# Output projection node tile by node tile, with four resident weight quarters, inside the edge-count build

## The chip, the cores and the metric

The kernel runs on one core of one Trainium2 chip. Its time is the device time of one launch in microseconds (us); below 2211.28 us for the kernel before, the median of three runs. TensorE (PE) multiplies matrices, VectorE (DVE), ScalarE (ACT) and GpSimd (POOL) do elementwise work, SyncE (SP) here only issues DMAs. Each engine works through its own list of instructions in order and waits on semaphores where the code says so.

## The reference, cut to what matters

Two layers over 1250 nodes with 1024 features and 20000 edges. The part that the change touches is in layer 0: the attention output is normalized, multiplied by a 1024x1024 matrix and added to the node features, and a second branch multiplies the features by a graph matrix built from the edges.

```python
h = jnp.einsum('nd,od->no', x, W) + b            # L0 gnn; self edges are appended to row and col
deg = jnp.zeros((num_nodes,), dtype=h.dtype).at[row].add(1.0)
norm = deg_inv_sqrt[row] * deg_inv_sqrt[col]
out = jax.ops.segment_sum(norm[:, None] * h[col], row, num_segments=num_nodes)
...
normed = (out - mu) / jnp.sqrt(var + EPS) * gamma + beta      # L0 mix
return normed @ W_out + b_out
```

All products are made in float16 pairs: an operand is split in a high and a low part, and each product is three matmuls (high-high, high-low, low-high).

## The kernel before

The nodes are 10 tiles of 128 (`NT`, `TN`), the features 8 blocks of 128 (`KD`). The stage in question, from about 776 us to 962 us of the span, does two things side by side:

- The edge-count build. The sorted edges come in 118 slices (`NST`). For each slice PE multiplies one-hot matrices (4 matmuls, "a stage" of the loop here, `st`); ACT copies the result out of PSUM (`rw`, counted by `rows_out`); DVE adds it to the count matrix `Bc` (`add_rows`, counted by `b_free`). DVE also makes the one-hots, for two stages at a time (`hot`, five instructions, counted by `oh_ready`).
- The output projection. One unit is one node tile times one quarter of `W_out` (256 columns): 24 matmuls of 128x256. There are 40 units, named u. `OUTS_AT` lists after which stage each stands. PE makes it into bank 2 or 3 of PSUM, DVE adds it to `X` (a "unit sum", counted by `evac`).

A weight quarter is loaded as float32 into `wst` by SP (`load`, which waits on `w_split` until the quarter before has been split), copied to float16 high by ACT (`weights_high`) and made into the low part by DVE (`weights_low`, which counts `w_split`). There are two slots for split quarters, so the order of the units is quarter by quarter: ten node tiles for quarter 0, then ten for quarter 1, and so on.

Ahead of the first stage ACT and POOL each clear half of `Bc` (`bc_clear`). After the last stage a serial chain leads to the next stage, the gather (`agg0`): DVE sums the degrees and adds two count rows (`both`), PE transposes them (`turn`), DVE scales (`make`), ACT and POOL split the result in `ATh` and `ATl`, and PE begins the gather with 60 matmuls for each node tile. The gather reads `G0`, 5 MB that SP loads in one DMA once all 40 units are through, since it lies where the projection's input `OT0h`, `OT0l` lay.

The order of all of it is written by hand in the code of each engine. SP's queue has the loads in program order too, and each waits for those ahead of it to be issued.

Of the kernel before, what the change touches and what calls it, by code (L numbers as in the profile page):

```python
# [8 lines left out]
F16 = mybir.dt.float16  # L9
# [3 lines left out]
ALU = mybir.AluOpType  # L13
# [95 lines left out]
def build_program(nc, A, out):  # L109

    with ExitStack() as ctx:
# [204 lines left out]
        z_normed, z_gained = sem("z_normed"), sem("z_gained")  # L316
        gb_loaded, g_hi, g_back = sem("gb_loaded"), sem("g_hi"), sem("g_back")
        g_saved = [sem(f"g_saved{r}") for r in range(4)]
# [18 lines left out]
        b_loaded = sem("b_loaded")  # L337
        xr_loaded = [sem(f"xr_loaded{i}") for i in range(NT)]
        x_biased = sem("x_biased")
# [176 lines left out]

        def unit(pe, n, t, o, xh, xl, i):
# [3 lines left out]
            at = slice(i * TN, (i + 1) * TN)  # L521
            x, m = three(o, [(xh[:, k, at], xl[:, k, at], Wh[:, k], Wl[:, k]) for k in range(KD)])
            if t % NT == 0:
                x.then_inc(slot_begun, 1)
            m.then_inc(mm_done, 1)

        def g_unit(pe, u):
            T = TILE0["gnn0"] + u
            wait_ring(pe, T)
            unit(pe, SLOT0["gnn0"] + u // NT, u, ps[0:TN, T % 4, 0:256], XTh, XTl, u % NT)  # L530

# [340 lines left out]
        def _(pe):  # L872
# [61 lines left out]
            def gather(i, c):  # L934
                s, T = i % 2, T0 + 2 * i + c
                if c == 0:
                    pe.wait_ge(at_lo, i + 1)
                wait_ring(pe, T)
                _, m = three(ps[0:TN, T % 4, :],
                             [(ATh[s][:, k], ATl[s][:, k], G0[:, 0, k, c * 512:(c + 1) * 512],  # L940
                               G0[:, 1, k, c * 512:(c + 1) * 512]) for k in range(NT)])
                m.then_inc(mm_done, 1)
# [22 lines left out]
            turn(0)  # L965
            pe.wait_ge(g_back, 16)
            for i in range(NT - 1):
# [262 lines left out]
        def _(act):  # L1230
# [199 lines left out]
        def _(pool):  # L1430
# [217 lines left out]
        def _(sp):  # L1648
# [3 lines left out]
            for i in range(NT):  # L1652
                if i == NT - 1:
                    sp.wait_ge(const_ready, 1)
                sp.dma_start(X[0:rows_of(i), i], x_rows(i)).then_inc(xr_loaded[i], 16)
                if i == 1:
# [56 lines left out]
            sp.dma_start(bias_g, A["L0_gnn_b"].unsqueeze(0).to_broadcast([TN, DIM])).then_inc(gb_loaded, 16)  # L1713
            sp.wait_ge(b_loaded, 32)
            sp.dma_start(bias_o, A["L0_mix_b_out"].unsqueeze(0).to_broadcast([TN, DIM])).then_inc(b_loaded, 16)
            sp.wait_ge(fold_out, NGR)
            sp.dma_start(es.rearrange("p j q c -> p (j q) c").rearrange("p (t q) c -> p t q c", q=2),
                         edges_d.rearrange("(t p q) c -> p t q c", p=128, q=2)).then_inc(e_back, 16)
            for i in range(NT):
# [4 lines left out]
                if i in (1, 3):  # L1724
                    load(sp, 14 + i // 2, wst[:, 0:2048], A["w_gnn0"][2 + i // 2])
                if i == 6:
                    load(sp, 16, wst[:, 0:2048], A["w_out0"][0])
                sp.wait_ge(turn_done, TURN0["lnO"] + i + 1)
                sp.dma_start(X[0:rows_of(i), i], x_rows(i)).then_inc(xr_loaded[i], 16)
            for n in (17, 18, 19):  # L1730
                load(sp, n, wst[:, 0:2048], A["w_out0"][n - SLOT0["mix0_out"]])
            load(sp, SLOT0["ffn_up"], wsti[:, 0:2048], A["w_up0"][0])
            sp.wait_ge(mm_done, TILE0["agg0"])
# [78 lines left out]
        def _(dve):  # L1812
# [161 lines left out]
            for i in range(NT):  # L1974
                dve.wait_ge(z_gained, i + 1)
                zz = z[i % 2][:, 0:DIM]
                v.tensor_tensor(zz, zz, bcast[1], ALU.add).then_inc(z_ready, 1)
                if i in (0, 3, 6, 8):
                    weights_low(dve, 13 + (i + 1) // 3)
                for u in range(4 * i, 4 * i + 4):  # L1980
                    g_sum(u)
# [4 lines left out]
                g_low(4 * i + 3)  # L1986
                turn_lows(dve, "lnO", i, i % 2, OT0h, OT0l, OS0)
                if i == NT - 4:
# [8 lines left out]
            def add_rows(st):  # L1997
# [4 lines left out]
                rows = flat[:, bass.ds(off, BW)]  # L2002
                v.tensor_tensor(rows, rows, rw[st % 4], ALU.add).then_inc(b_free, 1)
            hot(1)
            dve.wait_ge(bc_clear, 2)
            dve.wait_ge(st_moved, 16)
            for st in range(NST):
                if st % 2 == 0 and st // 2 + 2 < NST // 2:
                    hot(st // 2 + 2)
                if st in OUTS_AT:  # L2010
                    u = OUTS_AT.index(st)
                    if u < NT:
                        dve.wait_ge(xr_loaded[u], 32)
                    dve.wait_ge(mm_done, TILE0["mix0_out"] + u + 1)
                    x = X[:, u % NT, u // NT * 256:u // NT * 256 + 256]
                    stt(x, out_bank(u), 1.0 / (OS0 * WS), x, ALU.mult, ALU.add).then_inc(evac, 1)
# [506 lines left out]
```

## Time and profile before

| | |
|---|---|
| time, median of 3 runs (lowest to highest) | 2211.28 us (2209.93 to 2212.87) |
| profiled execution, first to last instruction (span) | 2207.7 us |
| PE busy | 2068.7 us, 94% |
| DVE busy | 1234.6 us, 56% |
| ACT busy | 725.6 us, 33% |
| POOL busy | 1003.1 us, 45% |

The page gives the profiled execution as its span only; what lies around the span is the 3.6 us by which the median of the runs exceeds it. A share is an average over all stages. The stage of the change has other shares than the whole.

### The profile page before, as it was taken

Reading aid. Unit: us, or ns where it says so; the run is one execution under the profiler, and the core shown is the slowest. Engines: PE = TensorE matmul, PEld = TensorE weight load, DVE = VectorE, ACT = ScalarE, POOL = GpSimd, SP = SyncE. Lnnn points to the kernel's source line nnn. Section 1 sums busy time; section 2 is a strip of 40 time slices with the busy share of each in tenths; the row PEclk is TensorE's granted clock in tenths of the full one; section 3 lists DMA queues with packets and bytes.
Section 4 is the critical chain, followed back from the end, with each engine's and each line's share of the span. In section 5 each row is a group of like instructions: output and inputs, shape, how many; then the busy total and the mean of one; then the engine's idle time right before and its main releaser. Section 6 shows DMA issues by size and latency. Waiting matters only on the chain.

```text
span 2207.7 us, 41128 instructions
## 1 busy us (share of the span) xinstructions
PE 2068.7 (94%) x16448; PEld 1423.1 (64%) x16448; DVE 1234.6 (56%) x2250; ACT 725.6 (33%) x1080; POOL 1003.1 (45%) x783
## 2 busy tenths in 40 slices
PE   7989999999998999969999999999999998977997
PEld 6555564474457977734545577747877887865765
DVE  6784555547566699965534622546555633374332
ACT  5243444435563354320230512312222220052332
POOL 3218777878773200025503873049334422333554
PEclk9999999999999999979999999999999999987999
DMA  4302333324156311060001021211211212376886
GB/s 160 89 20 56 87 91 74 91 69 104 23 140 158 113 54 39 13 200 20 20 0 47 28 73 38 88 39 34 66 41 40 55 29 63 140 304 180 153 153 106
DMA packets 128120, 182.14 MB, mean 83 GB/s; under 512 B 52066, under 2 KB 97257, under 8 KB 121679
## 3 DMA queue, kind: packets, MB, share of 16 engines
q1 hardware_dynamic: 111102, 150.87, 22.6%
q0 software_dynamic: 16848, 28.90, 7.8%
q8 instruction: 119, 1.95, 0.4%
q14 instruction: 51, 0.41, 0.1%
HBM read 120.82 MB, written 53.49 MB: 79 GB/s over the span
## 4 chain that ended last, share of the span: by engine, by line
PE 76%; POOL 9%; DVE 6%; issue 5%; DMA 2%; ACT 1%; SPq 0%; DVEq 0%; POOLq 0%; ACTq 0%
PE ps L494 19%; PE ps L497 19%; PE ps L496 19%; POOL edges_sorted L1532 4%; PE pt L717 2%; DVE RB L798 2%; PE ps L699 2%; PE pt L912 2%; PE pt L479 1%; POOL WR L1524 1%; POOL WR L1523 1%; POOL WR L1520 1%; PE pt L1155 1%; PE ps L1174 1%; PE ps L1175 1%
## 5 line engine op out<-in xcount | busy, mean ns | idle before, releaser
L494 PE MATMUL ps<-WR,RB 128*128 128x256 f16 (+2 forms) x2248 | 630.2, 280 | 6.9 <-DVE SR L1817 3.5
L496 PE MATMUL ps<-WR,RB 128*128 128x256 f16 (+2 forms) x2248 | 629.8, 280 | 0.0
L497 PE MATMUL ps<-WR,RB 128*128 128x256 f16 (+2 forms) x2248 | 629.7, 280 | 0.0
L494 PEld LDWEIGHTS ps<-WR,RB 128*128 128x128 f16 x2248 | 220.2, 98 | 52.7 <-DVE RB L446 3.1
L494 PE MATMUL ps<-RB,WR 128*128 128x512 f16 (+1 forms) x720 | 246.5, 342 | 8.0 <-DVE RB L446 7.4
L1532 POOL DMA_INDIRECT edges_sorted<-SR x160 | 199.9, 1250 | 117.4 <-DVE SR L1922 56.9
L497 PEld LDWEIGHTS ps<-WR,RB 128*128 128x128 f16 x2248 | 220.0, 98 | 42.5 <-issue 0.7
L497 PE MATMUL ps<-RB,WR 128*128 128x512 f16 (+1 forms) x720 | 246.4, 342 | 0.0
L496 PE MATMUL ps<-RB,WR 128*128 128x512 f16 (+1 forms) x720 | 246.4, 342 | 0.0
L496 PEld LDWEIGHTS ps<-WR,RB 128*128 128x128 f16 x2248 | 220.5, 98 | 39.7 <-issue 0.8
L1473 POOL TENSOR_TENSOR WR<-WR,units 128x3072 f32<-128x3072 f32 (+2 forms) x16 | 74.2, 4635 | 371.5 <-PE ps L494 317.3
L798 DVE SCALAR_TENSOR_TENSOR RB<-ps,SR 128x1024 f16<-128x1024 f32 (+2 forms) x120 | 121.5, 1022 | 45.0 <-ACT SR L760 44.4
L760 ACT ACTIVATE SR<-ps 128x1024 f16<-128x1024 f32 (+2 forms) x120 | 104.3, 869 | 88.7 <-PE ps L699 64.7
L2234 DVE TENSOR_TENSOR SR<-SR 128x128 f32<-128x128 f32 (+2 forms) x104 | 101.0, 971 | 44.8 <-ACT SR L1359 44.8
L1476 POOL TENSOR_TENSOR WR<-WR,units 128x3072 f16<-128x3072 f32 (+2 forms) x20 | 90.6, 4530 | 71.2 <-PE ps L494 48.9
L699 PE MATMUL ps<-RB 64*128 64x512 f16 (+2 forms) x960 | 111.7, 339 | 11.5 <-DVE RB L798 10.1
L1630 POOL DMA_INDIRECT out<-WR,SR x54 | 84.4, 1563 | 82.3 <-ACT WR L1412 69.3
L494 PEld LDWEIGHTS ps<-RB,WR 128*128 128x128 f16 x720 | 71.0, 99 | 66.9 <-issue 9.9
L460 ACT ACTIVATE SR<-RB,nbias,rstd 128x1024 f32<-128x1024 f32 x50 | 61.7, 1237 | 144.1 <-POOL nbias L441 144.1
L497 PEld LDWEIGHTS ps<-RB,WR 128*128 128x128 f16 x720 | 71.0, 99 | 57.7 <-issue 1.6
L496 PEld LDWEIGHTS ps<-RB,WR 128*128 128x128 f16 x720 | 71.0, 99 | 57.2 <-issue 1.4
L1520 POOL TENSOR_TENSOR WR<-WR,units 128x512 f32<-128x512 f32 x64 | 69.0, 1078 | 81.8 <-DMA WR<-in_w_moe 81.4
(348 smaller groups left out, 4041.9 us busy)
## 6 DMA issues: line engine op xcount, KB each, us to landing
WR<-in_w_moe SPq DMA_DIRECT2D x64, 256.0 KB, 3.6
moe_split<-WR SPq DMA_DIRECT2D x128, 128.0 KB, 1.8
RB<-moe_split SPq DMA_DIRECT2D x8, 2048.0 KB, 15.6
WR<-in_w_mix SPq DMA_DIRECT2D x12, 1024.0 KB
WR<-in_w_mix SPq DMA_DIRECT2D x8, 1536.0 KB
RB<-in_x SPq DMA_DIRECT2D x18, 512.0 KB, 6.1
WR<-in_w_out SPq DMA_DIRECT2D x8, 1024.0 KB
RB<-counts SPq DMA_DIRECT2D x10, 640.0 KB, 4.8
```

What stands on the lines that cost most here:

```text
L494: m = nc.tensor.matmul(o, ah, bh, start=(k == 0), stop=False)
L496: nc.tensor.matmul(o, ah, bl, start=False, stop=False)
L497: m = nc.tensor.matmul(o, al, bh, start=False, stop=(k == n - 1))
L699: m = nc.tensor.matmul(bank[0:r, h, 0:w], k[HEAD[h], keys], x[HEAD[h], q], start=(n == 0), stop=(n == 2))
L760: nc.scalar.activation(Ph[u % 6][0:r, :, 0:w], score_bank(T, j)[0:r, :, 0:w], ACT.Relu).then_inc(hi_done, 2)
L798: nc.vector.scalar_tensor_tensor(Pl[u][0:r, :, 0:w], score_bank(T, j)[0:r, :, 0:w], 0.0, Ph[u][0:r, :, 0:w], ALU.max, ALU.subtract).then_i ...
L1473: ch.link(g.tensor_tensor(w, w, units[:, 2:3].to_broadcast([128, width]), ALU.mult))
L1476: ch.link(g.tensor_tensor(wh[s][:, 0:width], wst[:, 0:width], units[:, 3:4].to_broadcast([128, width]), ALU.mult))
L1520: ch.link(g.tensor_tensor(pst[s], pst[s], units[:, 2:3].to_broadcast([128, PIECE]), ALU.mult))
L1532: g.indirect_dma_start(edges_d, bass.IndirectOffsetOnAxis(pos[:, t:t + 1], 0), rec[:, t, :], None).then_inc(e_moved, 16)
L1630: g.indirect_dma_start(out2, bass.IndirectOffsetOnAxis(idx2[:, c, t:t + 1], 0), yo[t % 3][:, c * 512:(c + 1) * 512], None, compute_op=ALU. ...
L2234: v.tensor_tensor(o, vw(er[e]), vw(er[2 + e]), ALU.add).then_inc(k_done, 1)
```

## The change

`OUTS_AT` now has 36 entries, from stage 8 on, 2.75 stages apart (before: 40 entries from stage 1 on, 2.5 apart). The last four units stand behind the loop, on PE ahead of the first `turn`, and on DVE their sums stand between the two `both`, ahead of `make(0)`. A unit number u means node tile u // 4 and quarter u % 4, so the first four units need all four quarters. Quarters 0 to 3 lie in spare halves of the weight slots, in the two slots, and in the end and the beginning of `wst` itself.

The conversions therefore move to the front: the high copy of quarter 1 stands on ACT before its clear of `Bc`, that of quarter 2 after stage 1 and that of quarter 3 after stage 6; DVE makes the low parts before its wait for `bc_clear`, after stage 3 and after stage 8.

`OT0h` and `OT0l` are laid out by node tile, so that when the four units of a node tile are through, the 512 KB of `G0` for that tile can be loaded over them. SP issues ten such loads in place of the one. The load of the output bias and that of the next stage's weights move behind these ten, since `wst` is in use until the last unit.

```diff
-OUTS_AT = [5 * u // 2 + 1 for u in range(4 * NT)]
+OUTS_AT = [8 + 11 * u // 4 for u in range(4 * NT - 4)]
...
-        OT0h, OT0l = R2(0, F16, KD, NP), R2(20480, F16, KD, NP)
+        OT0h, OT0l = R2(0, F16, NT, KD, TN), R2(20480, F16, NT, KD, TN)
...
+        tails = WR(12288, F16, 2, 2, 3072)[:, :, :, 2048:3072]
...
+        def quarter(c):
+            if c == 0:
+                return tails[:, 0], tails[:, 1]
+            if c == 3:
+                return (wst_h.rearrange("p (b n) -> p b n", b=2) for wst_h in (WR(8192, F16, 2048), WR(0, F16, 2048)))
+            return (w[c - 1][:, 0:2048].rearrange("p (b n) -> p b n", b=2) for w in (wh, wl))
+
+        def quarter_high(act, c):
+
+            act.wait_ge(w_loaded, 16 * (SLOT0["mix0_out"] + c) + 16)
...
+        def out_unit(pe, u):
+
+            i, c = divmod(u, 4)
+            if u < 4:
+                pe.wait_ge(w_split, SLOT0["mix0_out"] + c + 1)
+            if u >= 2:
+                pe.wait_ge(evac, TILE0["mix0_out"] + u - 1)
...
                 if st in OUTS_AT:
-                    u = OUTS_AT.index(st)
-                    if u >= 2:
-                        pe.wait_ge(evac, T0 + u - 1)
-                    unit(pe, SLOT0["mix0_out"] + u // NT, u, out_bank(u), OT0h, OT0l, u % NT)
+                    out_unit(pe, OUTS_AT.index(st))
+            for u in range(4 * NT - 4, 4 * NT):
+                out_unit(pe, u)
...
-                if i in (2, 5, 7):
+                if i in (2, 5):
                     weights_high(act, 14 + i // 3)
+                if i == 7:
+                    quarter_high(act, 0)
+            quarter_high(act, 1)
...
-                if st - 1 in (OUTS_AT[0], OUTS_AT[NT], OUTS_AT[2 * NT]):
-                    weights_high(act, 17 + OUTS_AT.index(st - 1) // NT)
+                if st == 1:
+                    quarter_high(act, 2)
+                if st == 6:
+                    quarter_high(act, 3)
...
-            sp.dma_start(G0, g0_d).then_inc(g_back, 16)
+            for i in range(NT):
+                sp.wait_ge(mm_done, TILE0["mix0_out"] + 4 * i + 4)
+                sp.dma_start(G0[:, :, i], g0_d[:, :, i]).then_inc(rows_loaded[i], 16)
+            sp.wait_ge(b_loaded, 32)
+            sp.dma_start(bias_o, A["L0_mix_b_out"].unsqueeze(0).to_broadcast([TN, DIM])).then_inc(b_loaded, 16)
+            load(sp, SLOT0["ffn_up"], wsti[:, 0:2048], A["w_up0"][0])
...
             hot(1)
+            quarter_low(dve, 1)
             dve.wait_ge(bc_clear, 2)
...
-                if st - 3 in (OUTS_AT[0], OUTS_AT[NT], OUTS_AT[2 * NT]):
-                    weights_low(dve, 17 + OUTS_AT.index(st - 3) // NT)
+                if st == 3:
+                    quarter_low(dve, 2)
+                if st == 8:
+                    quarter_low(dve, 3)
...
             both(0)
-            both(1)
+            for u in range(4 * NT - 4, 4 * NT - 2):
+                out_sum(u)
             dve.wait_ge(dis_ready, 1)
...
+            both(1)
+            for u in range(4 * NT - 2, 4 * NT):
+                out_sum(u)
             make(0)
```

ACT at the front of the loop, before. The clear of `Bc` is the row of 128x6400, a copy of a stage's result has 128x626, and a high copy of a weight quarter 128x2048.

```order
L1266 ACTIVATE RB<-pt 128x8x128 [waits turn_done]
L1272 ACTIVATE RB<-kvs 128x6400 [waits mm_done]
L1280 ACTIVATE SR<-ps 128x626 [waits g_saved3,g_saved2,oh_used,g_saved1,g_saved0]
L1280 ACTIVATE SR<-pt 128x626 [waits oh_used] x2
L598 ACTIVATE WR<-WR 128x2048 [waits w_loaded,slot_begun]
L1280 ACTIVATE SR<-ps 128x626 [waits oh_used]
L1280 ACTIVATE SR<-pt 128x626 [waits b_free,oh_used] x2
```

And now:

```order
L1304 ACTIVATE RB<-pt 128x1024 [waits turn_done]
L544 ACTIVATE WR<-WR 128x2048 [waits slot_begun,w_loaded]
L1314 ACTIVATE RB<-kvs 128x6400 [waits mm_done]
L1322 ACTIVATE SR<-ps 128x626 [waits g_saved3,g_saved2,oh_used,g_saved1,g_saved0]
L1322 ACTIVATE SR<-pt 128x626 [waits oh_used]
L544 ACTIVATE WR<-WR 128x2048 [waits mm_done,w_loaded]
L1322 ACTIVATE SR<-pt 128x626 [waits oh_used]
L1322 ACTIVATE SR<-ps 128x626 [waits oh_used]
L1322 ACTIVATE SR<-pt 128x626 [waits b_free,oh_used] x2
L1322 ACTIVATE SR<-ps 128x626 [waits b_free,oh_used]
L544 ACTIVATE WR<-WR 128x2048 [waits mm_done,w_loaded]
```

A high copy (L544) now stands ahead of the clear; a second one stands behind the copy of stage 1 and a third behind the copy of stage 6, each waiting on `w_loaded`.

DVE behind the last stage, before. The first row is the last `add_rows`; the 128x1250 rows are `both`, the 128x1024 row is the first part of `make(0)`.

```order
L2003 TENSOR_TENSOR RB<-RB,SR 128x626
L2022 TENSOR_REDUCE deg<-RB 128x10 [waits b_free]
L2023 TENSOR_SCALAR deg<-deg 128x10 [waits dve_chain]
L2025 MEMSET SR 128x30
L2025 MEMSET SR 128x30 [waits dve_chain]
L2031 TENSOR_TENSOR SR<-RB 128x1250 [waits turn_done,dve_chain]
L2031 TENSOR_TENSOR SR<-RB 128x1250 [waits turn_done]
L2069 TENSOR_SCALAR deg<-deg 128x10 [waits dis_ready]
L2070 TENSOR_SCALAR deg<-deg 128x10 [waits dve_chain]
L2038 TENSOR_TENSOR SR<-pt,deg 128x1024 [waits turn_done,dve_chain]
```

And now, from the row behind the last `add_rows` on:

```order
L2077 TENSOR_REDUCE deg<-RB 128x10 [waits b_free]
L2078 TENSOR_SCALAR deg<-deg 128x10 [waits dve_chain]
L2080 MEMSET SR 128x30
L2080 MEMSET SR 128x30 [waits dve_chain]
L2086 TENSOR_TENSOR SR<-RB 128x1250 [waits turn_done,dve_chain]
L1862 SCALAR_TENSOR_TENSOR RB<-ps,RB 128x256 [waits mm_done,rows_loaded9]
L1862 SCALAR_TENSOR_TENSOR RB<-ps,RB 128x256 [waits mm_done]
L2125 TENSOR_SCALAR deg<-deg 128x10 [waits dis_ready]
L2126 TENSOR_SCALAR deg<-deg 128x10 [waits dve_chain]
L2086 TENSOR_TENSOR SR<-RB 128x1250 [waits turn_done,dve_chain]
L1862 SCALAR_TENSOR_TENSOR RB<-ps,RB 128x256 [waits mm_done] x2
L2093 TENSOR_TENSOR SR<-pt,deg 128x1024 [waits turn_done]
```

Four unit sums (128x256) have come in between `both(0)` and `make(0)`, two ahead of `both(1)` and two behind it.

SP from the last load of node features on, before:

```order
L1729 DMA RB<-in_x 98x1024 [waits turn_done]
L385 DMA WR<-in_w_out0 128x2048 [waits w_split] x3
L385 DMA WR<-in_w_up0 128x2048 [waits w_split]
L1736 DMA RB<-g0_split 128x20480 [waits g_saved2,g_saved1,g_saved3,g_saved0,mm_done]
L1739 DMA counts<-RB 2560x2x625 [waits deg_ready,b_free]
```

And now:

```order
L1771 DMA RB<-in_x 98x1024 [waits turn_done]
L386 DMA WR<-in_w_out0 128x2048 [waits w_split] x2
L1778 DMA RB<-g0_split 128x2x1024 [waits g_saved3,g_saved2,mm_done,g_saved1,g_saved0]
L1778 DMA RB<-g0_split 128x2x1024 [waits mm_done] x9
L1780 DMA WR<-in_L0_mix_b_out 128x1024 [waits b_loaded]
L386 DMA WR<-in_w_up0 128x2048 [waits w_split]
L1784 DMA counts<-RB 2560x2x625 [waits deg_ready,b_free]
```

One quarter fewer is loaded here, the load of `G0` is in ten parts, each waiting for its units, and the bias and the `w_up0` load stand behind them and ahead of the store of the counts.

## Rows read from the trace of the kernel before

**Rows 1.** The page, its first line.
```profile
span 2207.7 us, 41128 instructions
```

**Rows 2.** Busy time by windows: whole loop: length; PE, PEld, DVE, ACT, POOL; clock, DMA share, GB/s.
```profile
776.50:961.94 185.44, 173.60 (x1432) 129.71 (x1432) 175.01 (x451) 84.58 (x122) 2.25 (x1) 0.96 0.15 55
```

**Rows 3.** Groups by line, DVE in that window: count, busy us, mean ns, idle before, releasers.
```profile
L2003 DVE TENSOR_TENSOR RB<-RB,SR 128x626 f16 x118 | 56.9, 482 | 9.3 <-DVE RB L2003 7.8 <-issue 0.9 <-ACT SR L1280 0.5
...
L1817 DVE SCALAR_TENSOR_TENSOR RB<-ps,RB 128x256 f32<-128x256 f32 x40 | 16.7, 418 | 0.2 <-PE ps L497 0.2
L603 DVE SCALAR_TENSOR_TENSOR WR<-WR 128x2048 f16<-128x2048 f32 x3 | 6.9, 2285 | 0.0
```

**Rows 4.** Timeline, DVE in the loop: start us, duration us, engine, line, operation.
```profile
827.20 0.49 DVE L2003 TENSOR_TENSOR RB<-RB,SR 128x626 f16 x1 [0.20 <-DVE RB L2003]
...
831.58 0.48 DVE L2003 TENSOR_TENSOR RB<-RB,SR 128x626 f16 x1
...
915.94 0.49 DVE L2003 TENSOR_TENSOR RB<-RB,SR 128x626 f16 x1 [0.20 <-DVE RB L2003]
...
919.12 0.49 DVE L2003 TENSOR_TENSOR RB<-RB,SR 128x626 f16 x1 [0.20 <-DVE RB L2003]
...
946.06 0.48 DVE L2003 TENSOR_TENSOR RB<-RB,SR 128x626 f16 x1
946.74 0.49 DVE L2003 TENSOR_TENSOR RB<-RB,SR 128x626 f16 x1 [0.20 <-DVE RB L2003]
...
948.92 0.48 DVE L2003 TENSOR_TENSOR RB<-RB,SR 128x626 f16 x1
```

**Rows 5.** Timeline of all engines where the loop begins.
```profile
775.08 5.53 ACT L1272 ACTIVATE RB<-kvs 128x6400 f32<-128x6400 f32 x1
...
775.94 15.30 SPq L385 DMA_DIRECT2D WR<-in_w_out  x2
...
776.98 2.82 DVE L1972 TENSOR_SCALAR SR<-SR 128x625 f16<-128x625 f16 x4
...
780.51 0.68 ACT L1280 ACTIVATE SR<-ps 128x626 f16<-128x626 f32 x1
...
782.43 0.47 DVE L2003 TENSOR_TENSOR RB<-RB,SR 128x626 f16 x1
...
782.99 1.91 ACT L598 ACTIVATE WR<-WR 128x2048 f16<-128x2048 f32 x1 [0.64 <-DMA WR<-in_w_out]
```

**Rows 6.** Timeline, SP and ACT: one weight quarter loaded alone and its copy.
```profile
660.09 0.33 SPq L385 DMA_DIRECT2D WR<-in_w_gnn  x1
...
665.10 1.91 ACT L598 ACTIVATE WR<-WR 128x2048 f16<-128x2048 f32 x1 [2.72 <-DMA WR<-in_w_gnn]
```

**Rows 7.** Timeline of all engines where the loop ends and the gather begins.
```profile
957.84 1.25 PE L912 MATMUL ps<-SR 128*128 128x512 f16 x4
...
961.45 0.49 DVE L2003 TENSOR_TENSOR RB<-RB,SR 128x626 f16 x1 [0.33 <-DVE RB L2003]
...
962.62 2.83 DVE L2031 TENSOR_TENSOR SR<-RB 128x1250 f32<-128x1250 int16 x2
...
964.18 2.37 PE L930 MATMUL pt<-ident,SR 128*128 128x128 f32 x10 [5.09 <-issue]
...
966.23 1.23 DVE L2038 TENSOR_TENSOR SR<-pt,deg 128x1024 f32<-128x1024 f32 x1 [0.49 <-PE pt L930]
...
972.29 0.61 PE L494 MATMUL ps<-RB,SR 128*128 128x512 f16 x1 [2.32 <-POOL SR L1562]
```

**Rows 8.** Busy time and granted clock by windows of 2 us, near the end.
```profile
942.00:944.00 2.00, 1.43 (x6) 0.64 (x7) 1.80 (x7) 0.50 (x2) 0.00 (x0) 0.51 1.06 451
976.00:978.00 2.00, 2.00 (x10) 0.91 (x9) 0.06 (x1) 0.07 (x1) 1.85 (x1) 0.96 1.08 254
```

**Rows 9.** Timeline, PE within a unit: first matmul of two successive threes.
```profile
934.88 0.27 PE L494 MATMUL ps<-WR,RB 128*128 128x256 f16 x1
...
935.21 0.27 PE L494 MATMUL ps<-WR,RB 128*128 128x256 f16 x1
```

More of the change, by code:

```diff
@@ L337, in build_program @@
         b_loaded = sem("b_loaded")
-        xr_loaded = [sem(f"xr_loaded{i}") for i in range(NT)]
+        rows_loaded = [sem(f"rows_loaded{i}") for i in range(NT)]
         x_biased = sem("x_biased")
@@ L515, in gemm_nodes, with g_unit @@
                     m.then_inc(mm_done, 1)
-        def unit(pe, n, t, o, xh, xl, i):
+        def g_unit(pe, u):
+            T, n, at = TILE0["gnn0"] + u, SLOT0["gnn0"] + u // NT, slice(u % NT * TN, (u % NT + 1) * TN)
+            wait_ring(pe, T)
             pe.wait_ge(w_split, n + 1)
             Wh, Wl = (w[n % 2][:, 0:2048].rearrange("p (k n) -> p k n", k=KD) for w in (wh, wl))
-            at = slice(i * TN, (i + 1) * TN)
-            x, m = three(o, [(xh[:, k, at], xl[:, k, at], Wh[:, k], Wl[:, k]) for k in range(KD)])
-            if t % NT == 0:
+            x, m = three(ps[0:TN, T % 4, 0:256], [(XTh[:, k, at], XTl[:, k, at], Wh[:, k], Wl[:, k])
+                                                  for k in range(KD)])
+            if u % NT == 0:
@@ new lines, in quarter_high, with quarter_low @@
+        def quarter_high(act, c):
+            act.wait_ge(w_loaded, 16 * (SLOT0["mix0_out"] + c) + 16)
+            if c == 1:
+                act.wait_ge(slot_begun, SLOT0["mix0_out"])
+            if c >= 2:
+                act.wait_ge(mm_done, TILE0["mix0_out"])
+            hi, _ = quarter(c)
+            nc.scalar.activation(hi, wst[:, 0:2048].rearrange("p (b n) -> p b n", b=2), ACT.Copy,
+                                 scale=WS).then_inc(w_high, 1)
+        def quarter_low(dve, c):
+            dve.wait_ge(w_high, SLOT0["mix0_out"] + c - 1)
+            hi, lo = quarter(c)
+            nc.vector.scalar_tensor_tensor(lo, wst[:, 0:2048].rearrange("p (b n) -> p b n", b=2), WS, hi, ALU.mult,
+                                           ALU.subtract).then_inc(w_split, 1)
@@ new lines, in out_unit @@
+        def out_unit(pe, u):
[4 more added lines that the diff above has]
+                pe.wait_ge(evac, TILE0["mix0_out"] + u - 1)
+            Wh, Wl = (w.rearrange("p b (k n) -> p b k n", k=4) for w in quarter(c))
+            x, m = three(out_bank(u), [(OT0h[:, i, k], OT0l[:, i, k], Wh[:, k // 4, k % 4], Wl[:, k // 4, k % 4])
+                                       for k in range(KD)])
+            if u < 4:
+                x.then_inc(slot_begun, 1)
+            m.then_inc(mm_done, 1)
@@ L938, in gather @@
                 wait_ring(pe, T)
-                _, m = three(ps[0:TN, T % 4, :],
-                             [(ATh[s][:, k], ATl[s][:, k], G0[:, 0, k, c * 512:(c + 1) * 512],
-                               G0[:, 1, k, c * 512:(c + 1) * 512]) for k in range(NT)])
+                for k in range(NT):
+                    if T == T0:
+                        pe.wait_ge(rows_loaded[k], 48)
+                    o, cols = ps[0:TN, T % 4, :], slice(c * 512, (c + 1) * 512)
+                    nc.tensor.matmul(o, ATh[s][:, k], G0[:, 0, k, cols], start=(k == 0), stop=False)
+                    nc.tensor.matmul(o, ATh[s][:, k], G0[:, 1, k, cols], start=False, stop=False)
+                    m = nc.tensor.matmul(o, ATl[s][:, k], G0[:, 0, k, cols], start=False, stop=(k == NT - 1))
                 m.then_inc(mm_done, 1)
@@ L965, in _ @@
             turn(0)
-            pe.wait_ge(g_back, 16)
             for i in range(NT - 1):
@@ L1725, in _ @@
                     load(sp, 14 + i // 2, wst[:, 0:2048], A["w_gnn0"][2 + i // 2])
-                if i == 6:
-                    load(sp, 16, wst[:, 0:2048], A["w_out0"][0])
+                if i in (6, 8):
+                    load(sp, 13 + i // 2, wst[:, 0:2048], A["w_out0"][i // 2 - 3])
                 sp.wait_ge(turn_done, TURN0["lnO"] + i + 1)
-                sp.dma_start(X[0:rows_of(i), i], x_rows(i)).then_inc(xr_loaded[i], 16)
-            for n in (17, 18, 19):
+                sp.dma_start(X[0:rows_of(i), i], x_rows(i)).then_inc(rows_loaded[i], 16)
+            for n in (18, 19):
                 load(sp, n, wst[:, 0:2048], A["w_out0"][n - SLOT0["mix0_out"]])
-            load(sp, SLOT0["ffn_up"], wsti[:, 0:2048], A["w_up0"][0])
-            sp.wait_ge(mm_done, TILE0["agg0"])
             for r in range(4):
                 sp.wait_ge(g_saved[r], 16 * NT)
-            sp.dma_start(G0, g0_d).then_inc(g_back, 16)
+            for i in range(NT):
[4 more added lines that the diff above has]
+            load(sp, SLOT0["ffn_up"], wsti[:, 0:2048], A["w_up0"][0])
             sp.wait_ge(b_free, NST)
@@ L1986, in _ @@
                 g_low(4 * i + 3)
-                turn_lows(dve, "lnO", i, i % 2, OT0h, OT0l, OS0)
+                dve.wait_ge(turn_hi, i + (H0["lnO"] + 1))
+                hi, lo = (a[:, i].rearrange("p (b k) n -> p b k n", b=2) for a in (OT0h, OT0l))
+                stt(lo, turn_view(i % 2), OS0, hi, ALU.mult, ALU.subtract).then_inc(turn_lo, 1)
                 if i == NT - 4:
@@ L2003, in add_rows, with out_sum @@
                 v.tensor_tensor(rows, rows, rw[st % 4], ALU.add).then_inc(b_free, 1)
+            def out_sum(u):
+                i, c = divmod(u, 4)
+                if c == 0:
+                    dve.wait_ge(rows_loaded[i], 32)
+                dve.wait_ge(mm_done, TILE0["mix0_out"] + u + 1)
+                x = X[:, i, c * 256:c * 256 + 256]
+                stt(x, out_bank(u), 1.0 / (OS0 * WS), x, ALU.mult, ALU.add).then_inc(evac, 1)
             hot(1)
+            quarter_low(dve, 1)
             dve.wait_ge(bc_clear, 2)
```

28 lines of the change are left out of this document (10 added, 18 removed).

## The prediction

> **What bounds the kernel now.** I read the page first: the span is 2207.7 us [rows 1], and the median of the runs lies 3.6 us above it (2211.28). The sum below is made in the profiled execution's time and then added to the median. I then read the window of the loop. It lasts 185.4 us; PE is busy for 173.6 of them and DVE for 175.0 [rows 2], so the shares don't tell which of the two sets the pace. The groups by line for DVE do. In the loop DVE idles 9.3 us ahead of its 118 count additions, 7.8 of them on its own previous addition, and 0.2 us ahead of the 40 unit sums, which are what waits for PE [rows 3]. An engine that hardly ever waits for another one sets the pace. DVE's timeline gives its prices [rows 4]: a pair of stages without a unit takes 2.86 us (946.06 to 948.92), of which 2.18 run from the pair's second addition to the next first one (946.74 to 948.92); a pair with a unit sum behind the one-hots takes 3.18 us (915.94 to 919.12); with a low copy in it the 2.18 become 4.38 (827.20 to 831.58). So a unit costs DVE 0.32 us where it stands behind the one-hots and about 0.1 where it fills the 0.20 us wait between two additions, 0.2 on average, and a low copy costs 2.2.
>
> PE's own bill is near by. Three matmuls of a unit take 0.33 us [rows 9], so a unit of 24 takes 2.6. Before, the last unit stands behind stage 98, and behind it come 19 stages in which PE is half idle. The change spreads the units over these.
>
> **The loop, term by term.** The pace is DVE's, so what counts is what DVE does and what it is made to wait for.
>
> Units: four of 40 leave the loop, 4 x 0.2 = -0.8 us. Low copies: three stood in the loop, two stand there now, -2.2. The one of quarter 1 now stands ahead of the wait for `bc_clear`, where DVE is idle anyway: the one-hots there end at 776.98 + 2.82 = 779.80, the copy takes 2.3 [rows 3], so it ends at 782.1, and the clear ends later than that (next term). Odd waits: of the 9.3 + 0.2 us of idle, 1.7 is not DVE's own chain [rows 3]. With fewer units for each stage PE is further ahead, and I take 1.0 of it as gone, with 0 and 1.7 as ends.
>
> Start: ACT has a high copy of 1.9 us [rows 6] ahead of its clear of 5.53 us (from 775.08 to 780.61 [rows 5]). Its weights were asked for one node tile earlier and have landed. The clear ends at 782.5 and the first addition (782.43 in the row) comes at 784.3: +1.9.
>
> Stall at stage 2: quarter 2 can be loaded only when the low copy of quarter 1 has freed `wst`, at 782.1. A quarter loaded alone takes 5.0 us from issue to the start of its copy (660.09 to 665.10, ACT idle on the DMA before it [rows 6]); the one loaded at 775.94, with other traffic, took 7.0 (to 782.99 [rows 5]). So it lands at 787.1, ACT's copy ends at 789.0. Behind that copy on ACT, in order, is the result of stage 2, 0.7 us [rows 5], at 789.7. DVE wants it for addition 2, which by the price list comes at 784.3 + 2.9 = 787.2. It waits +2.6 (4.6 if the load takes 7.0).
>
> Stall at stage 7: addition 3 is at 790.5, the low copy of quarter 2 ends at 793.2, only then quarter 3 is loaded, lands at 798.2, is copied by 800.1, and the result of stage 7, queued behind it on ACT, is out at 800.8. Addition 7 by the price list would be at 790.5 + 2.2 + 2 x 2.86 = 798.4: +2.4 (4.4 at the slow load). Here the kernel before had the conversions one at a time and tens of us apart, so nobody waited for them, but for 0.64 us.
>
> The Trainium skill bears on this term, and speaks against the change. "DMA: Bandwidth & Descriptors", section Rules for kernel authors, says to issue a DMA early and wait late. Its section Anatomy of one DMA fits a transfer as 2.0 us plus its bytes over 436 GB/s, which gives an estimate of 4.4 us for the 1 MiB of a quarter. By that both stalls would be 0.6 shorter and the whole sum 1.2 us smaller; the row above has 5.0.
>
> Loop: 1.9 + 2.6 + 2.4 - 0.8 - 2.2 - 1.0 = +2.9 us. Whether PE keeps up with that is nearly a tie. Of its 173.6 us [rows 2] the 40 units take 104, which leaves 0.6 for each of 118 stages; two units in 5.5 stages are then 8.5 us, at most, since the last stages ran at half clock and count too high. DVE takes 5.5 x 1.43 + 2 x 0.2 = 8.3. PE starts ahead by the eight stages without units and falls back by 0.2 at most each time, so the tie costs nothing in 18 such steps; if it did, up to 3.
>
> **Behind the loop.** Before, the last addition starts at 961.45, `both(0)` at 962.62, the transposes at 964.18, `make(0)` at 966.23 and the first gather matmul at 972.29 [rows 7]: 10.8 us from the last addition, in series. With the change PE has four units in its list ahead of the transposes. Set the last addition to 0. PE is through with the last stage at 957.84 + 1.25, that is at -2.4; two units end at +2.9. The next unit writes the bank of the first one and waits for its sum, which on DVE stands behind `both(0)`: that one starts at 1.2 and takes half of 2.83, so the sum runs from 2.7 to 3.1. The last two units take from 3.1 to 8.4. Only now the transposes begin: eight of them 1.1 us at the full clock (2.0 before, at half), `make(0)` at 9.6, and from there to the gather 972.29 - 966.23 = 6.1 as before: 15.7. That is +4.8 us. The sums of the last two units end at 8.8 and delay nothing. What the units gain, PE work in an idle stretch, is lost since they stand ahead of the chain and not beside it.
>
> The clock: PE is at 0.51 of full speed (1.2 of 2.4 GHz) after some us of sparse work [rows 8], and the gather before starts at half and is at 0.96 in the window from 976 on [rows 8]. Ahead of the new gather PE is dense until 9.7 and nearly idle for 6 us. I take it that the gather starts at half again, as before, which changes nothing. If it stays at full, 1.9 us come back (the 3.8 us from 972.29 to about 976.1, halved). If the four units themselves start at half, +1.6.
>
> The loads: the last part of `G0` is asked for when the last unit is through, at 8.4, and is wanted 27 matmuls behind the gather's start at 15.7. The bias comes behind it; POOL wants it behind its first split, and its next split is due only when PE has made the 60 matmuls of the first node tile. SP's store of the counts starts some 10 us later, and what waits for it stands behind the whole gather. I count all three at 0, with +1 if the bias lands late enough to hold up POOL's second split.
>
> Sum: +2.9 + 4.8 = +7.7 us. The profile would show a span of 2215.4, and the time is 2211.28 + 7.7 = 2219.0.
>
> **Rivals.**
>
> (A) PE sets the pace of the loop. For it: PE is busy 94% of it, as DVE is, and all the 10.4 us of four units (4 x 2.6 [rows 9]) leave it. Then the loop is 10.4 shorter, the conversions hide in the first eight stages that have no unit, and the tail still costs 4.8: -5.6, 2205.7 us, faster. Against it: DVE waits only 0.2 us for units [rows 3]. It decides from where DVE would wait for PE several us in a loop. 0.14.
>
> (B) The two stalls don't come, since loads land within the slack that ACT's run ahead of DVE gives (up to three stages). Then the loop is -2.1 and the whole +2.7, 2214.0; with the gather at full clock 2212.1. Against: the slack is used in my working already. 0.17.
>
> (C) Both loads take the 7.0 us of the busy queue, and the four units start at half clock: +7.7 + 4.0 + 1.6 = +13.3, 2224.6. Against: no other traffic is in the queue then. 0.09.
>
> **How the numbers follow.** My forecast has 0.60; its own range is 2216 to 2222 (the 1.2 and 1.9 us below, odd waits and clock above). What a measurement of this kernel can tell from no change is about 0.2%, 4.4 us: from 2206.9 to 2215.7. Faster is A, 0.14. Within are B, most of 0.17, and a tenth of mine: 0.24. Slower is the rest, 0.62. The range for 8 in 10 runs from 2210, which leaves out A, to 2224, which leaves out the upper half of C.
>
> **What would show it.** Right: ACT idle for some 3 us ahead of its second and third high copies in the loop, ended by the DMA, and DVE idle about as long ahead of additions 2 and 7; behind these, pairs of stages at 2.9 to 3.2 us, as before; the last addition 2 to 4 us later than 961.45; the first transpose over 8 us behind it, the first gather matmul some 15.7 behind it, with PE dense on four units between; from the gather on every stage as before, shifted. Wrong: the last addition well ahead of 960 (A or B), additions 2 and 7 without a wait (B), or a stage behind the gather that takes up the shift because something other than PE bounds it.

## The result, and the profile after

| kernel | median of the runs | lowest to highest | ratio to before (95% interval) | span of the profiled run |
|---|---|---|---|---|
| before | 2208.41 us, 11 runs | 2207.11 to 2212.87 | 1 | 2207.7 us |
| after | 2216.11 us, 11 runs | 2212.66 to 2219.14 | 1.0031 (1.0024 to 1.0039) | 2214.3 us |

The change makes the kernel slower by 0.31%, that is 6.9 us (5.3 to 8.6). The forecast was +7.7 us and 2219.0 us.

The window of the whole loop, from its first matmul to the end of the last count addition, after; it answers to [rows 2]. Columns are the length, then busy time with the count of instructions for PE, PEld, DVE, ACT and POOL, then clock, DMA share and GB/s:

```profile
778.20:966.52 188.32, 171.45 (x1370) 125.08 (x1371) 173.63 (x447) 84.82 (x122) 2.25 (x1) 0.94 0.13 40
```

The loop is 188.3 us long where it was 185.4, and DVE is busy for 1.4 us less. The groups by line of DVE say where the 2.9 us are. These answer to [rows 3]: idle time ahead of the instruction and what ended it stand last. Their window here is 776 to 970 us, so the first two of the four unit sums behind the loop are in it, 36 of the loop and 2.

```profile
L2052 DVE TENSOR_TENSOR RB<-RB,SR 128x626 f16 x118 | 56.9, 482 | 14.2 <-DVE RB L2052 9.1 <-ACT SR L1322 5.2
...
L1862 DVE SCALAR_TENSOR_TENSOR RB<-ps,RB 128x256 f32<-128x256 f32 x38 | 15.8, 418 | 0.0
```

DVE now idles 14.2 us ahead of its 118 additions: 9.1 on its own previous one and 5.2 on ACT, which was 0.5 in [rows 3]. In the loop it never waits for a unit's matmuls.

Who ACT waited for is in the timeline of the loop's beginning, after, which answers to [rows 5] (start, duration, engine, line, operation; in brackets the idle time before it and what ended it):

```profile
776.78 1.90 ACT L544 ACTIVATE WR<-WR 128x2048 f16<-128x2048 f32 x1
...
778.58 5.53 ACT L1314 ACTIVATE RB<-kvs 128x6400 f32<-128x6400 f32 x1
...
781.42 2.28 DVE L551 SCALAR_TENSOR_TENSOR WR<-WR 128x2048 f16<-128x2048 f32 x1
783.73 11.24 SPq L386 DMA_DIRECT2D WR<-in_w_out  x2
...
785.92 0.48 DVE L2052 TENSOR_TENSOR RB<-RB,SR 128x626 f16 x1
...
788.49 1.91 ACT L544 ACTIVATE WR<-WR 128x2048 f16<-128x2048 f32 x1 [3.22 <-DMA WR<-in_w_out]
...
791.11 0.49 DVE L2052 TENSOR_TENSOR RB<-RB,SR 128x626 f16 x1 [2.24 <-ACT SR L1322]
...
799.60 1.91 ACT L544 ACTIVATE WR<-WR 128x2048 f16<-128x2048 f32 x1 [5.57 <-DMA WR<-in_w_out]
...
802.22 0.49 DVE L2052 TENSOR_TENSOR RB<-RB,SR 128x626 f16 x1 [2.58 <-ACT SR L1322]
```

The first high copy (776.78) stands ahead of the clear, the low copy of quarter 1 (781.42) is followed at once by the load of quarter 2 (783.73), and the copy of that (788.49) waited 3.22 us for it. Addition 2 (791.11) then waited 2.24 us for ACT. The same happens once more: the copy at 799.60 waited 5.57 us for its load, and addition 7 at 802.22 waited 2.58 us.

The loop's end and the gather's beginning, after, answer to [rows 7]:

```profile
962.31 0.70 PE L948 MATMUL ps<-SR 128*128 128x512 f16 x4
...
966.03 0.49 DVE L2052 TENSOR_TENSOR RB<-RB,SR 128x626 f16 x1 [0.33 <-DVE RB L2052]
...
967.20 1.46 DVE L2086 TENSOR_TENSOR SR<-RB 128x1250 f32<-128x1250 int16 x1
...
968.58 0.75 DVE L1862 SCALAR_TENSOR_TENSOR RB<-ps,RB 128x256 f32<-128x256 f32 x2
...
969.05 0.28 PE L495 MATMUL ps<-WR,RB 128*128 128x256 f16 x1 [0.80 <-DVE RB L1862]
...
974.30 1.26 PE L965 MATMUL pt<-ident,SR 128*128 128x128 f32 x10
...
975.38 1.23 DVE L2093 TENSOR_TENSOR SR<-pt,deg 128x1024 f32<-128x1024 f32 x1 [0.45 <-PE pt L965]
...
981.44 0.61 PE L978 MATMUL ps<-RB,SR 128*128 128x512 f16 x1 [3.41 <-POOL SR L1606]
```

From the last addition (966.03) to the first gather matmul (981.44) it is 15.4 us; before, 961.45 to 972.29, 10.8. PE begins the third of the four units at 969.05, behind the sum of the first one (968.58), and the transposes only at 974.30.

The granted clock in 2 us windows, after, answers to [rows 8] (it is the third number from the end of a row):

```profile
984.00:986.00 2.00, 2.00 (x6) 0.73 (x5) 1.21 (x1) 1.22 (x1) 0.70 (x1) 0.50 1.08 296
986.00:988.00 2.00, 2.00 (x10) 0.88 (x9) 0.00 (x0) 0.00 (x0) 2.00 (x2) 0.98 1.08 265
```

The gather begins at half the clock, as before, and is at 0.98 from 986 on.

The first gather matmul comes 9.2 us later than before (981.44 against 972.29) and the sums of the gather 9.5 us later, since PE makes its first gather matmuls at half the clock for 4.6 us (to 986.1) where it was 3.8 (to 976.1). The whole span grew by 6.6 only. The difference is outside of the stage. Ahead of the loop 1.7 us were lost (its first matmul is at 776.50 before and at 778.20 after); seven other profiles of this case, whose code ahead of the loop is that of the changed kernel, have it from 775.4 to 778.6, so 1.7 us is within their spread. Between 1116 and 1166 us of the kernel before, 3.2 us came back. The windows of the second one, before and after, begin at the same work and are of equal length:

```profile
1116.00:1136.00 20.00, 17.54 (x82) 8.62 (x82) 7.09 (x13) 8.33 (x8) 1.07 (x4) 0.91 0.00 1
1136.00:1166.00 30.00, 25.07 (x129) 13.88 (x128) 9.64 (x11) 7.54 (x8) 0.00 (x0) 0.91 0.00 1
```

```profile
1125.50:1145.50 20.00, 17.53 (x92) 9.06 (x91) 7.12 (x13) 8.34 (x8) 1.07 (x4) 1.00 0.00 1
1145.50:1175.50 30.00, 25.08 (x149) 15.56 (x148) 9.64 (x11) 7.90 (x9) 0.00 (x0) 0.94 0.00 1
```

In the same time PE has 92 and 149 matmuls where it had 82 and 129. The granted clock is 0.91 and 0.91 before, 1.00 and 0.94 after, and nothing of the change is in that part; why the clock differs there, no run shows. The single profiled runs differ by such drops of the clock, so I read each term inside the stage, between its own marks, and take the whole from the ratios.

### The profile page after: what moved, and what is told of

It is laid out like the page before. It is cut to its first block, busy times and chain, and to the rows that moved or that the text cites. A ratio compares the mean times of both kernels' runs of the same rounds, so it can differ in the third digit from the quotient of the medians.

```text
span 2214.3 us, 41100 instructions
## 1 busy us (share of the span) xinstructions
PE 2068.9 (93%) x16448; PEld 1421.6 (64%) x16448; DVE 1234.3 (56%) x2250; ACT 726.0 (33%) x1080; POOL 1003.3 (45%) x783
## 4 chain that ended last, share of the span: by engine, by line
PE 78%; DVE 7%; POOL 6%; issue 5%; DMA 2%; ACT 1%; DVEq 0%; SPq 0%; POOLq 0%; ACTq 0%
PE ps L495 17%; PE ps L498 17%; PE ps L497 17%; PE pt L753 3%; DVE RB L834 2%; PE ps L735 2%; PE ps L978 2%; PE ps L979 2%; PE ps L980 2%; POOL edges_sorted L1576 2%; PE pt L480 1%; PE pt L948 1%; PE pt L1193 1%; PE ps L1213 1%; PE ps L1212 1%
## 5 line engine op out<-in xcount | busy, mean ns | idle before, releaser
L1524 POOL TENSOR_TENSOR WR<-WR 128x3072 f16<-128x3072 f32 (+2 forms) x20 | 104.8, 5241 | 1.3
```

What stands on the lines that cost most here:

```text
L1524: g.tensor_tensor(wl[s][:, 0:width], wst[:, 0:width], wh[s][:, 0:width], ALU.subtract).then_inc(w_split, 1)
```

## The experiments

All start from the changed kernel. Two lengths are read from each profile: from the first to the last count addition (the loop), and from the last one to the first gather matmul (the tail).

| kernel | median, us | ratio to before (95% interval) | loop, us | tail, us |
|---|---|---|---|---|
| before | 2208.41 | 1 | 179.0 | 10.8 |
| after | 2216.11 | 1.0031 (1.0024 to 1.0039) | 180.1 | 15.4 |
| e1_tail | 2206.90 | 0.9995 (0.9986 to 1.0004) | 180.2 | 10.2 |
| e2_conv | 2213.52 | 1.0020 (1.0011 to 1.0029) | 177.9 | 15.4 |
| e3_both | 2205.48 | 0.9987 (0.9978 to 0.9996) | 178.2 | 10.2 |
| e4_half | 2212.04 | 1.0017 (1.0007 to 1.0027) | 179.8 | 12.8 |
| e5_small | 2210.27 | 1.0004 (0.9994 to 1.0014) | 175.3 | 15.4 |
| e6_one | 2225.08 | 1.0071 (1.0052 to 1.0089) | 180.2 | 24.3 |
| e7_conv2 | 2201.97 | 0.9970 (0.9957 to 0.9982) | 176.1 | 10.2 |
| e8_early | 2204.20 | 0.9969 (0.9958 to 0.9980) | 175.5 | 10.2 |

The ratios compare each kernel with runs of the kernel before on its own chip, whose median was 2208.6 us for the first four and 2209.9 for the last four. The first three have 11 runs each, e4_half and e5_small 8, e6_one only 2, e7_conv2 6 and e8_early 7, so differences of 1 or 2 us between two of them are not told apart. The two lengths are from one profile each.

**e1_tail: the last two units behind the first transposes.**

```diff
-            for u in range(4 * NT - 4, 4 * NT):
+            for u in range(4 * NT - 4, 4 * NT - 2):
                 out_unit(pe, u)
...
             turn(0)
+            for u in range(4 * NT - 2, 4 * NT):
+                out_unit(pe, u)
...
+            make(0)
             both(1)
             for u in range(4 * NT - 2, 4 * NT):
                 out_sum(u)
-            make(0)
```

> The changed kernel with the last two units (38, 39) behind the first transposes on TensorE instead of ahead of them, and their sums behind make(0) and both(1) on VectorE. My theory (the four units stand in series with the chain to the gather): two units fit ahead of the chain and two beside it, so the first gather matmul comes 10 to 11 us behind the last addition instead of 15.4, and starts at the full clock; 5 to 7 us below the changed kernel, 2209 to 2211. Rival (the gather is late since its rows, the bias or the split come late, not because of the order): no change, 2216. Rival (the 15.4 is the clock's): half of it goes, about 2 us.

Its timeline behind the last addition, which starts at 965.22:

```profile
967.95 1.28 PE L965 MATMUL pt<-ident,SR 128*128 128x128 f32 x10 [0.53 <-issue]
...
974.30 1.26 PE L965 MATMUL pt<-ident,SR 128*128 128x128 f32 x10
975.40 0.38 PE L978 MATMUL ps<-RB,SR 128*128 128x512 f16 x1
```

POOL there, and the 2 us window in which the gather begins (the clock is the third number from the end):

```profile
972.52 2.61 POOL L1608 TENSOR_TENSOR SR<-SR 128x1280 f16<-128x1280 f32 x1 [4.30 <-ACT SR L1335]
980.70 2.34 POOL L1612 TENSOR_TENSOR RB<-RB,WR 128x1024 f32<-128x1024 f32 x1 [5.56 <-DMA WR<-in_L_mix_b_out]
```

```profile
974.00:976.00 2.00, 2.00 (x18) 1.66 (x16) 1.04 (x2) 0.00 (x0) 1.14 (x1) 1.00 0.09 14
```

The transposes begin 2.7 us behind the last addition, the second ones at 974.30, and the gather at 975.40, 10.2 us behind it. POOL's split, the end of the serial chain, is done at 975.13, so the two units (PE, 969.2 to 974.3) lie beside the chain. The gather's first matmul takes 0.38 us, against 0.61 in the kernel before and after: PE has had no gap to speak of, and the granted clock is 1.00. The tail is 5.2 us shorter. Some 2 us more come from the clock: the gather's second sum comes 13.2 us behind its first matmul (988.55) where it was 15.4 in the changed kernel (996.88). The whole gains 0.36% on the changed kernel, 8 us, a little more than the 5 to 7 that I had expected; from the kernel before it is not told apart. The rival that something else holds up the gather falls, and so does the one that the 15.4 is the clock's: the 5.2 us are gained before the gather begins. POOL now waits 5.56 us for the bias (980.70), which costs nothing here: PE does not wait for it.

**e2_conv: the conversions of quarters 2 and 3 later.**

```diff
-                if st == 1:
+                if st == 5:
                     quarter_high(act, 2)
-                if st == 6:
+                if st == 12:
                     quarter_high(act, 3)
...
-                if st == 3:
+                if st == 6:
                     quarter_low(dve, 2)
-                if st == 8:
+                if st == 13:
                     quarter_low(dve, 3)
```

> The changed kernel with the high copies of quarters 2 and 3 behind stages 5 and 12 instead of 1 and 6 on ScalarE, the low copies behind additions 6 and 13 instead of 3 and 8. Units stay where they are. My theory (each conversion blocks ScalarE's results until a load that was only just asked for lands): the waits of 2.2 and 2.6 us ahead of additions 2 and 7 go, at most 1 us of new wait comes; 4 to 5 us below the changed kernel, 2211 to 2212. Rival (TensorE's late first units set the pace there, the stall only hides it): less than 1.5 us gained.

By addition 14, when both low copies are through in both kernels, it had won 4.9 us on the changed kernel, counted from the first addition. That is the whole of the two stalls, and it is more than the rival allows. By addition 24 only 2.2 were left. The group of the unit sums on DVE in the window 776 to 970, all of DVE's waits of more than 0.1 us for units in it, and the one long wait of PE from 795 to 822:

```profile
L1862 DVE SCALAR_TENSOR_TENSOR RB<-ps,RB 128x256 f32<-128x256 f32 x40 | 16.7, 418 | 3.8 <-PE ps L498 3.8
```

```profile
811.48 0.42 DVE L1862 SCALAR_TENSOR_TENSOR RB<-ps,RB 128x256 f32<-128x256 f32 x1 [0.64 <-PE ps L498]
...
819.41 0.42 DVE L1862 SCALAR_TENSOR_TENSOR RB<-ps,RB 128x256 f32<-128x256 f32 x1 [0.15 <-PE ps L498]
...
966.86 0.42 DVE L1862 SCALAR_TENSOR_TENSOR RB<-ps,RB 128x256 f32<-128x256 f32 x1 [0.78 <-PE ps L498]
969.48 0.42 DVE L1862 SCALAR_TENSOR_TENSOR RB<-ps,RB 128x256 f32<-128x256 f32 x1 [2.19 <-PE ps L498]
```

```profile
PE ps L495 <- DVE WR L551: 3.4, 1, 3.4
```

```profile
804.00:806.00 2.00, 0.00 (x0) 0.00 (x0) 2.00 (x2) 0.07 (x1) 0.00 (x0) 0.59 0.00 0
...
808.00:810.00 2.00, 2.00 (x11) 1.44 (x10) 1.80 (x5) 0.00 (x0) 0.00 (x0) 0.50 0.00 0
```

Of the 3.8 us that DVE waited for units only 0.8 lie in the loop. The other 3.0 are ahead of the last two sums, behind the last addition (961.01), where the changed kernel has the same waits (0.78 and 2.20). The loss in the loop is that from addition 14 to 24 DVE takes 17.7 us where it took 15.0: it idles 0.8 us ahead of unit sums and 1.9 ahead of additions, together 2.1 more than in the changed kernel. PE had waited 3.4 us for the low copy of quarter 3, which I had set behind addition 13 with its unit at stage 16, and ran at half clock behind that gap, so that this unit took 4.9 us in place of 2.5. I take this late unit for the cause of DVE's idle time there; of the 1.9 us ahead of additions 1.2 have no releaser in the profile, so this link is argued and not shown row by row. The stall had partly turned into a new one of my own making. The expectation of 4 to 5 us is missed; 2.4 us by the ratios are what is left of it.

**e3_both: both edits.** Its code is that of the two above.

> Both edits together: the last two units behind the first transposes, and the later conversions. My theory has the two terms independent: 9 to 11 us below the changed kernel, 2205 to 2207, that is 1 to 3 us faster than the kernel before. If one wait only takes the place of the other, it is no better than the better of the two alone.

The two terms add up: 0.9987 against 1.0031 is 9.7 us below the changed kernel, and the kernel is 0.13% faster than the one before (0.04% to 0.22%).

**e4_half: units of half the matmuls.**

```diff
-                                       for k in range(KD)])
+                                       for k in range(KD // 2)])
```

> The changed kernel with four of the eight feature blocks left out of each unit, so 12 matmuls in place of 24 (half of the projection is left out). If VectorE sets the pace of the loop, as I hold: the time from the first to the last count addition changes by less than 1.5 us, and the whole kernel gains only what the two last units lose behind the last addition, 2.6 us, so 2212 to 2214 (less if the clock then stays down). If TensorE sets the pace: 36 units x 1.3 = 47 us less in the loop.

The loop is 179.8 us against 180.1. Half of the units' matmuls are gone, 432 in the loop, which is some 47 us at full clock. PE's busy time in the window of the loop falls by less, from 171.5 to 137.8 us, since the granted clock is 0.88 there and was 0.94. The loop is 0.3 us shorter all the same: DVE sets the pace. The tail is 12.8 us, 2.6 below the changed kernel's, which is the half of the two last units, as the working of the tail has it. The whole is 3.1 us below the changed kernel by the ratios.

**e5_small: the loads of quarters 2 and 3 small.**

```diff
-                load(sp, n, wst[:, 0:2048], A["w_out0"][n - SLOT0["mix0_out"]])
+                load(sp, n, wst[:, 0:256], A["w_out0"][n - SLOT0["mix0_out"]][:, 0:256])
```

> The changed kernel, only that the loads of quarters 2 and 3 bring 256 of 2048 columns (the rest of these quarters is left out). Everything else, all copies too, stays. If the waits at additions 2 and 7 are the loads' landing, they shrink by what a load of 128 KB lands sooner than one of 1 MB, 2 to 3 us each: both waits nearly go, and the loop is 4 to 5 us shorter. If they are ScalarE's 1.9 us copies or the one-hots, they stay.

```profile
L2052 DVE TENSOR_TENSOR RB<-RB,SR 128x626 f16 x118 | 56.8, 482 | 9.6 <-DVE RB L2052 9.2 <-ACT SR L1322 0.3
```

DVE's wait for ACT ahead of the additions is 0.3 us where it was 5.2, and the loop is 4.8 us shorter. ACT's copies are still there, at their places and of their size. So the two waits are the landing of the loads, not the copies. The whole is 6.0 us below the changed kernel by the ratios.

**e6_one: one load of `G0` behind the last unit.**

```diff
-            for i in range(NT):
-                sp.wait_ge(mm_done, TILE0["mix0_out"] + 4 * i + 4)
-                sp.dma_start(G0[:, :, i], g0_d[:, :, i]).then_inc(rows_loaded[i], 16)
+            sp.wait_ge(mm_done, TILE0["mix0_out"] + 4 * NT)
+            sp.dma_start(G0, g0_d).then_inc(rows_loaded[NT], 16)
```

> The changed kernel with one load of all of G0 (5 MB) behind the last unit in place of ten loads in the loop. My theory (the loads tile by tile hide the transfer, the order costs the tail): the gather then waits for the landing, 17 to 20 us behind the last unit instead of 7.2, so 10 to 13 us more than the changed kernel, 2226 to 2229. Rival (the ten loads disturb the loop and are themselves a part of the loss): a shorter loop and less than 8 us more in all.

```profile
990.81 0.58 PE L978 MATMUL ps<-RB,SR 128*128 128x512 f16 x1 [11.98 <-DMA RB<-g_split]
```

PE waits 11.98 us for the load and the tail is 24.3 us; the gather begins some 16 us behind the last unit, a little sooner than the 17 to 20 that I expected. The loop has the same length as with the ten loads (180.2 and 180.1), so these do not lengthen it, and the rival's shorter loop is not there. Without them the units behind the loop would have cost some 9 us more. The whole is 8.8 us above the changed kernel by the ratios, a little under my 10; with two runs this can be from 4 to 13.

**e7_conv2: the last two units as in e1_tail, the conversions in between.** High copies behind stages 4 and 10, low copies behind additions 5 and 11. Its expectation counts 3.8 us of waits for unit sums; as shown above, 0.8 of them were in the loop.

> The last two units behind the first transposes (as in the run with that edit alone), and the high copies of quarters 2 and 3 behind stages 4 and 10, the low copies behind additions 5 and 11, that is one and two stages earlier than in the run with later conversions. There TensorE waited 3.4 us for the low copy of quarter 3, ran at half clock after it, and VectorE waited 3.8 us for unit sums. My theory (that wait came from my placing of the low copy of quarter 3): it goes, 2 to 3 us below the kernel with both edits, 2202.5 to 2204 where the kernel before has 2208.6. Rival (the cause is the clock at the first units, wherever the copy stands): no change, 2205.5.

```profile
L2054 DVE TENSOR_TENSOR RB<-RB,SR 128x626 f16 x118 | 56.8, 482 | 10.1 <-DVE RB L2054 8.8 <-ACT SR L1324 0.9 <-issue 0.4
...
L1864 DVE SCALAR_TENSOR_TENSOR RB<-ps,RB 128x256 f32<-128x256 f32 x39 | 16.2, 418 | 0.0
```

The clock behind the low copy of quarter 3:

```profile
808.00:810.00 2.00, 2.00 (x13) 1.39 (x12) 2.00 (x6) 0.69 (x1) 0.00 (x0) 0.57 0.00 0
```

In the loop DVE waits neither for units (0.0) nor, by more than 0.9 us, for ACT. The loop is 176.1 us, 2.1 below e3_both, and PE has no wait for a low copy in it. The clock falls here too (0.57 at 808), but DVE does not come to wait for a unit by it, so the rival, that the cause is the clock wherever the copy stands, falls. With 0.9970 (0.9957 to 0.9982) the kernel is faster than both the one before and the changed one, by 6.6 us and 13.5 us. The 3.7 us to e3_both by the ratios are a little more than the 2 to 3 expected; the intervals of the two touch, so it is the loop that tells them apart, and it shows 2.1. The two profiles can't tell where the rest is: e7_conv2's loop begins 2.5 us later, and behind 1113 us it gains 4.8 us, where its granted clock up to 1300 is 0.99 against 0.96, far from the stage.

**e8_early: the high copy of quarter 1 ahead of the last copy of branch h.** The edit stands on top of that of e7_conv2.

```diff
                 for u in range(4 * i, 4 * i + 4):
+                    if u == 4 * NT - 1:
+                        quarter_high(act, 1)
                     g_high(u)
...
-            quarter_high(act, 1)
             act.wait_ge(mm_done, TILE0["mix0_out"])
```

> As the kernel just above, and the high copy of quarter 1 moved ahead of the last high copy of the branch h (g_high of unit 39) on ScalarE, where it idles 2.2 us, so that it no longer stands ahead of the clear. My theory: the first count addition comes 1.9 us earlier, and the kernel is 1.5 to 1.9 us below the one above. If the load of quarter 1 lands too late there, ScalarE's last copies wait for it and nothing is gained.

No gain can be told: 0.9969 against 0.9970, where I had expected 1.5 to 1.9 us. ACT and DVE at the start of its loop:

```profile
774.00 1.90 ACT L544 ACTIVATE WR<-WR 128x2048 f16<-128x2048 f32 x1
...
777.63 5.53 ACT L1317 ACTIVATE RB<-kvs 128x6400 f32<-128x6400 f32 x1
```

```profile
779.53 2.82 DVE L2020 TENSOR_SCALAR SR<-SR 128x625 f16<-128x625 f16 x4
782.27 2.28 DVE L551 SCALAR_TENSOR_TENSOR WR<-WR 128x2048 f16<-128x2048 f32 x1
784.47 0.68 DVE L2017 TENSOR_TENSOR SR<-SR 128x512 f16<-128x512 f16 x1
...
786.24 0.47 DVE L2055 TENSOR_TENSOR RB<-RB,SR 128x626 f16 x1
```

The clear is over at 783.16 now. The low copy of quarter 1 on DVE (782.27 for 2.28 us) ends at 784.5, and the one-hots (784.47) begin right behind it. In the changed kernel the low copy ended 0.4 us ahead of the clear, so behind the one wait stood the next, and only 0.4 us could be had. The first addition comes 7.2 us behind the loop's first matmul (779.04 to 786.24), and 7.7 in e7_conv2 (778.48 to 786.21).

## Why the prediction was right, step by step

*VectorE sets the pace of the loop.* Right, and shown by e4_half. Rival A, TensorE as the bound, would have made the loop tens of us shorter there (33.6 us by PE's busy time, some 47 at full clock). It sets it as long as PE's units are on time: in e2_conv a low copy for PE came late, and behind it the loop lost 2.7 us. The units are not spread over the whole of the loop's end, as the prediction has it: the last one in the loop stands behind stage 104, and 13 stages behind it have none.

*Start, +1.9.* Measured: the first addition is 7.72 us behind the loop's first matmul (778.20 to 785.92) and was 5.93 behind it (776.50 to 782.43), +1.8.

*Stall at addition 2, +2.6.* Measured 2.24. *Stall at addition 7, +2.4.* Measured 2.58. From issue to copy the loads took 4.8 us and about 5.0, as in [rows 6], not the 7.0 of [rows 5], so rival C had no ground. The prediction also estimates 4.4 us with the fit of the Trainium skill, "DMA: Bandwidth & Descriptors", section Anatomy of one DMA. That section gives the fit for DMAs issued by GpSimd, and SyncE issues these, so it says little of them; the measured 4.8 and 5.0 us are above it, and the 5.0 of [rows 6] was the nearer price. That the landing is the cause is shown by e5_small.

*Fewer units, one low copy less, fewer odd waits: -0.8, -2.2, -1.0.* Together -4.0. The length from first to last addition grew by 1.1 where the two stalls make 4.8, so these came to -3.7. How they share it was not taken apart. Of the odd waits (1.7) 0.3 is left, and DVE waits 1.3 us more on its own additions, since fewer unit sums fill these gaps.

*Tail, +4.8.* Measured +4.6. It came from the order on PE, as e1_tail shows, and the size from the two units that wait for a sum, as e4_half shows.

*The clock stays as before at the gather, 0.* Nearly right: the first matmul takes 0.61 us in both, but the half clock lasts 4.6 us where it was 3.8, which costs 0.4 us. The four units ran at the full level (1.00 in every window from 966 to 974).

*Rival B, no stalls.* Fell at additions 2 and 7.

Of the absolute time 2.9 us are off since the median of before, over more runs, is 2208.41 and not 2211.28; the difference itself, 7.7 forecast and 7.7 between the medians (6.9 by the ratio), held. By their own marks the terms make +1.8 + 1.1 + 4.6 = 7.5 us, and 7.9 with the clock at the gather. The mechanism held in each term that was measured by itself. That the sum is so near has luck in it: the single profiles differ by 3 us in other stages, the -1.0 for odd waits was a choice between 0 and 1.7, and the two stalls were missed by 0.4 and 0.2 us in opposite ways.

What I had not seen is how the fixes go on: the low copy of quarter 1, "where DVE is idle anyway", was only 0.4 us from being the bound itself (e8_early).

## What to carry to other kernels

Where one engine sets the pace of a loop, giving another engine a smoother share of work won nothing here, and what counts is what was moved into the first engine's way: here a copy queued ahead of results on ScalarE, waiting for a load that could only be issued when its buffer came free, 5 us before. Put such a copy as many stages behind the load's release as the load takes, and ahead of its first use by at least the producing copy, since a late one stalls the other side (e2_conv; in e7_conv2 places in between gave 4.0 us of loop back). Work that is to fill a gap must stand beside the serial chain that makes the gap: with two units ahead of the transposes and two behind them the tail is 10.2 us, where it was 10.8 without any; with four ahead of them it is 15.4.

## What the runs showed of the hardware

When units filled the gap ahead of the gather without a pause, its first matmul took 0.38 us in place of 0.61, and the granted clock there was 1.00 where it was 0.50; this is worth some 2 us by itself (13.2 against 15.4 us from the first gather matmul to the second sum). In e2_conv a gap of 3.4 us on PE in a stretch already thin of work came with windows at 0.59 and 0.50. A quarter's load of 1 MB, alone in the queue, took 4.8 and 5.0 us from issue to the start of the copy that waits for it. Ten loads of 512 KB during the loop changed the length of the loop by 0.1 us, no more than two profiles with the same loop differ by (180.1 in the changed kernel and 180.2 in e1_tail).
